# Weight loads in the order of use, vectors loaded as rows, and the second MLP's weights turned beside the first block, in an attention, MLP and LoRA-expert kernel on one core

## The chip, the cores and the metric

One core of a Trainium2 chip runs the whole program. Time is device microseconds (us) of one execution. What a measurement can tell from no change is said in the prediction. Engines are named as in the profile: PE is TensorE's matmul, PEld its weight load, DVE is VectorE, ACT is ScalarE, POOL is GpSimd, and SPq is the queue of SyncE, which issues every DMA of this kernel.

## What is computed

x is [4, 2048, 256] in float32: B = 4 batches, T = 2048 tokens, D = 256 features, 16 heads of 16. Weights are float32; MLP width is F = 1024.

```
xn  = ln(x) * g1 + b1n ;  q, k, v = split(xn @ w_in.T + b_in)
allowed = (idx % 8 == 0)[:, None] | (idx[:, None] == idx[None, :])
o   = softmax(where(allowed, q k^T / 4, -inf)) v
x1  = x + o @ w_out.T + b_out
x2  = x1 + gelu((ln(x1)*g2 + b2n) @ w1.T + b1) @ w2.T + b2
y   = layernorm(x + x2)
# second half: one of 8 experts is picked per token (top-1 of gate), each adds a rank-4 LoRA to the same wi
h   = relu(y @ wi.T + wi_b + (y @ A_e.T) @ B_e.T)
out = layernorm(y + h @ wo.T + wo_b)
```

Only one token in 8 attends to all tokens; the others see themselves alone, so for them attention is the value row itself. The kernel therefore works on a batch in 8 chunks of 256 tokens, one for each value of idx % 8. For chunks 1 to 7 attention is a matmul with v's and w_out's product; chunk 0 goes through real attention.

## The kernel before

**Precision.** Every float32 matmul is done as three matmuls of a reduced-width form (function `three`, lines 1459 to 1463 of the kernel): each operand is split into a high part, written by ACT, and a low part, written by DVE or POOL (exact value minus high part). So each weight tile needs a PE transpose ("turn"), one ACT copy, one DVE subtraction.

**Work of a batch.** It has two phases, *projection* and *attention*.
- Projection has three *pieces* for each of the 8 chunks (function `piece`): piece 0 normalises the next chunk (`pb`, DVE, tile xn) and multiplies k (`pk`, tile kst); piece 1 multiplies the first half of the value and x1 (`pv`), stores k (`stk`, 6 DMAs), takes the statistics of the chunk after next (`pa`, tile astats) and prepares x + the bias row on POOL (`xc`); piece 2 turns the next chunk (`pt`, tile xt), multiplies the second half, and completes x1 (`vx`: ACT writes vals, DVE adds into x1o, POOL sums x_s for the residual). `stx` stores x1 and x_s to DRAM, `ldx` loads a chunk of x into one of 4 buffers.
- Beside these run *items* of the two MLPs. A block is 512 tokens of one MLP ("M" the first, "F" the second) and has 8 items, one for each 128 of the 1024 hidden features: `up` (six matmuls of 512 columns, in the second MLP one more for the LoRA), gelu or relu on ACT (tile gel), `ev` (high part on ACT, low part on POOL: tile hid), and `dn` two items later. A block needs its rows normalised (`l2a`, `l2b`: tile x1in) and turned (`tn`: tile turned).
- `mx` steps (one PE pair and one DVE reduction each) find the maxima of the scores, in advance of the attention phase, which does `sc`, exponentials (tile prob) and `at` for 8 head pairs of 8 steps.

**Order.** `build_steps` writes one list of steps by hand; each engine walks through the whole list and issues its part in that order, so a wait in one step holds back everything behind it on that engine. `BANK` and `EARLIER` work out which PSUM bank a step uses and whom it waits for.

**The start.** SP loads four chunks of x, then all vectors and weights (`load_weights`, lines 719 to 740). Four vectors and wi_b are loaded as columns, one 4-byte element per partition (lines 722 to 724). Setup then makes the attention's weights: 6 of 25 groups (`wout`, `qk`, `vo`, `crow`), and the DVE products of `nwin` with the layer-norm bias (line 1148). The other 19 groups (`wt` steps 6 to 24: first MLP `upM`, `dnM`, second MLP `upF`, `dnF`, the gate `ga`, the LoRA `bst`) are put between the first 14 pieces, three or two ahead of each piece. The first MLP block of batch 0 starts after piece 14. It takes x1 of chunks 2 and 3 through DRAM: `stx` stores them and `l2l` loads them back into x1in. The first `up` waits for all 25 groups (line 1744 on):

```
                    if a == (0, 0):
                        pe.wait_ge(a_setup, A_SETUP)
                        pe.wait_ge(d_setup, D_SETUP)
```

The remaining 10 pieces go beside the first items, in shares of 3, 3, 2 and 2. The projection phase of batch 0 has three M blocks, 24 items, and 16 `mx` steps (`EARLY`).

## Time and profile before

| | |
|---|---|
| median of 3 runs | 1524.2 us (1523.08 to 1526.39) |
| the profiled execution | 1527.41 us, its span 1525.6 us |
| granted TensorE clock over the span | 0.985 of full speed |
| PE busy | 94% of the span |
| DVE, ACT, POOL busy | 55%, 48%, 43% |
| the first PE work after x's first chunk | at 15.77 us |
| the first `up` matmul | at 75.10 us |
| attention of batch 0 begins | at 179.91 us |

The page gives each engine's busy time over the span. It is an average over stages. The views read below are the table by stretches (busy time of each engine in a stretch, the granted clock, DMA share), the instructions in order of time, the groups by shape, and the waits (who waited for whom).

### The profile page before, as it was taken

The page shows a single profiled execution, that of the slowest core. Times are in us where ns is not written, and L with a number is a line of the kernel's source. Part 1 is how long each engine was busy: PE and PEld are TensorE (multiplying, and loading weights), DVE is VectorE, ACT ScalarE, POOL GpSimd, SP SyncE. Part 2 cuts the span into 40 slices and gives each one's busy share as a digit, 9 for nine tenths or more (in the row PEclk, how much of TensorE's full clock was granted, in tenths as well). Part 3 has the DMA queues.
Part 4 walks back from the last instruction along what each step waited for, and adds up shares of the span by engine and source line. Part 5 has one row for each costly group of instructions (what it writes and reads, how often), then busy time and mean ns, then how long its engine had stood idle before and what let it go on. Part 6 is the DMA issues. An engine that isn't in the chain of part 4 may idle for free.

```text
span 1525.6 us, 26433 instructions
## 1 busy us (share of the span) xinstructions
PE 1432.3 (94%) x10166; PEld 1074.9 (70%) x10166; DVE 839.0 (55%) x1791; ACT 725.3 (48%) x1071; POOL 649.9 (43%) x533
## 2 busy tenths in 40 slices
PE   5799899999989999999989999999999999999888
PEld 4587655568878765568878866566887765557777
DVE  6746466735645465545636545653575547663242
ACT  3353455554444555554434455455344455555433
POOL 2463321238754423235854431323775432133554
PEclk9899899999999999999999999999999999999999
DMA  8565123205561132212672213220567112310100
GB/s 199 172 194 118 36 47 75 53 15 191 188 143 55 36 76 47 53 42 77 201 200 60 77 25 75 51 54 15 163 203 156 56 36 48 76 25 28 43 15 28
DMA packets 102718, 131.55 MB, mean 86 GB/s; under 512 B 18889, under 2 KB 79249, under 8 KB 99473
## 3 DMA queue, kind: packets, MB, share of 16 engines
q1 hardware_dynamic: 102592, 129.86, 31.3%
q8 instruction: 81, 1.33, 0.4%
q14 instruction: 45, 0.36, 0.1%
HBM read 68.61 MB, written 61.10 MB: 85 GB/s over the span
## 4 chain that ended last, share of the span: by engine, by line
PE 72%; DVE 9%; POOL 6%; SPq 4%; DMA 4%; issue 3%; ACT 2%; POOLq 0%; DVEq 0%; ACTq 0%
PE ps L1461 17%; PE ps L1462 14%; PE ps L1463 14%; PE ps L1638 9%; PE ps L1627 6%; PE ps L1612 5%; DVE mx L1344 2%; PE ps L1683 2%; DMA k_d<-kst 2%; PE ps L1705 2%; DMA kslot<-ones_d 2%; SPq L770 1%; PE ps L1674 1%; POOL rows L961 1%; PE ps L1644 1%
## 5 line engine op out<-in xcount | busy, mean ns | idle before, releaser
L1344 DVE TENSOR_REDUCE mx<-ps 128x2 f32<-128x1024 f32 x256 | 313.3, 1224 | 265.9 <-PE ps L1612 252.2
L1082 ACT ACTIVATE prob<-ps 128x1024 f32<-128x1024 f32 x256 | 262.0, 1023 | 154.6 <-PE ps L1627 154.4
L974 POOL TENSOR_TENSOR hid0l<-gel,hid0h 128x512 fp32r<-128x512 f32 x86 | 112.5, 1308 | 232.2 <-ACT hid0h L1124 232.2
L974 POOL TENSOR_TENSOR hid1l<-gel,hid1h 128x512 fp32r<-128x512 f32 x85 | 111.1, 1307 | 228.0 <-ACT hid1h L1124 228.0
L974 POOL TENSOR_TENSOR hid2l<-gel,hid2h 128x512 fp32r<-128x512 f32 x85 | 111.1, 1307 | 217.3 <-ACT hid2h L1124 217.3
L1116 ACT ACTIVATE gel<-ps,cols 128x512 f32<-128x512 f32 x128 | 88.3, 690 | 197.4 <-PE ps L1463 188.8
L1638 PE MATMUL ps<-prob,vals 128*32 128x256 f32 x2048 | 165.4, 395 | 0.0
L1118 ACT ACTIVATE gel<-ps 128x512 f32<-128x512 f32 x128 | 76.6, 599 | 178.4 <-PE ps L1705 178.4
L1627 PE MATMUL ps<-qslot,kslot 50*128 50x256 f32 x1024 | 130.4, 333 | 7.1 <-ACT prob L1082 7.0
L1627 PEld LDWEIGHTS ps<-qslot,kslot 50*128 50x128 f32 x1024 | 77.2, 187 | 73.1 <-issue 47.9
L1612 PE MATMUL ps<-kslot,qslot 48*128 48x512 f32 x512 | 109.8, 425 | 9.6 <-DVE mx L1344 5.9
L1638 PEld LDWEIGHTS ps<-prob,vals 128*32 128x32 f32 x2048 | 40.5, 108 | 56.6 <-issue 47.1
L955 POOL TENSOR_TENSOR rstd<-vare,mhalf 128x4 f32<-128x4 f32 x47 | 50.2, 1068 | 69.5 <-DVE vare L1236 67.9
L961 POOL TENSOR_SCALAR rows<-rows,mv,rstd 128x256 f32<-128x256 f32 x60 | 73.6, 1238 | 0.0
L1419 DVE TENSOR_TENSOR rows<-rows,ps 128x512 f32<-128x512 f32 x62 | 40.6, 684 | 44.1 <-PE ps L1463 44.0
L1612 PEld LDWEIGHTS ps<-kslot,qslot 48*128 48x128 f32 x512 | 48.4, 185 | 22.0 <-DVE mx L1344 9.7
L1461 PE MATMUL ps<-turned1h,w1h 128*128 128x512 f32 x128 | 56.3, 440 | 5.6 <-DVE turned1l L1406 5.6
L1461 PE MATMUL ps<-turned0h,wih 128*128 128x512 f32 x128 | 60.2, 471 | 0.0
L1461 PE MATMUL ps<-turned0h,w1h 128*128 128x512 f32 x128 | 54.1, 422 | 4.0 <-DVE turned0l L1406 4.0
L1461 PE MATMUL ps<-turned1h,wih 128*128 128x512 f32 x128 | 57.7, 451 | 0.0
L911 POOL TENSOR_TENSOR arstd<-avare,mhalf 128x2 f32<-128x2 f32 x32 | 23.3, 729 | 76.7 <-DVE avare L1298 76.3
L1124 ACT ACTIVATE hid0h<-gel 128x512 fp32r<-128x512 f32 x86 | 54.2, 630 | 1.6
(238 smaller groups left out, 3968.5 us busy)
## 6 DMA issues: line engine op xcount, KB each, us to landing
k_d<-kst SPq DMA_DIRECT2D x192, 128.0 KB
kslot<-k_d SPq DMA_DIRECT2D x64, 384.0 KB
xin<-in_L_attn_x SPq DMA_DIRECT2D x32, 256.0 KB, 4.1
rows<-xs_d SPq DMA_DIRECT2D x16, 512.0 KB, 5.8
x1in<-x_d SPq DMA_DIRECT2D x15, 512.0 KB, 6.5
y_d<-rows SPq DMA_DIRECT2D x15, 512.0 KB, 3.1
rows<-y_d SPq DMA_DIRECT2D x15, 512.0 KB, 4.3
out<-rows SPq DMA_DIRECT2D x15, 512.0 KB, 4.5
```

The source lines that it names most:

```text
L961: nc.gpsimd.tensor_scalar(y[:, i, :], y[:, i, :], mv[:, k % 2, i, 0:1], rstd[:, k % 2, i:i + 1], ALU.subtract, ALU.mult).then_inc(final_do ...
L974: nc.gpsimd.tensor_tensor(hid[i % RING][1][:], gel[i % 2][:], hid[i % RING][0][:], ALU.subtract).then_inc(lo_done, 1)
L1082: nc.scalar.activation(prob[(n - 1) % 2][:].rearrange("p e i q -> p (e i q)"), ps[:, 0:2, :].rearrange("p a n -> p (a n)"), ACT.Exp).then_ ...
L1116: nc.scalar.activation(gel[i % 2][:], ps[:, UP, :], ACT.Gelu, bias=cols[:, B1C + f:B1C + f + 1]).then_inc(act_done, 1)
L1118: nc.scalar.activation(gel[i % 2][:], ps[:, UP, :], ACT.Relu).then_inc(act_done, 1)
L1344: nc.vector.tensor_reduce(best[:, :, j % NQ], ps[:, MX:MX + 2, :], AX.X, ALU.max).then_inc(maxr_done, 1)
L1461: mm(o, l[0], r[0], start=start, stop=False, skip_group_check=True)
L1462: mm(o, l[0], r[1], start=False, stop=False, skip_group_check=True)
L1463: return mm(o, l[1], r[0], start=False, stop=stop, skip_group_check=True)
L1612: last = mm(ps[:, MX + e, :], qslot[p % SLOTS][half, P * t:P * t + P], kslot[p % SLOTS][half, 512 * piece:512 * piece + 512], start=True, ...
L1627: last = mm(ps[:, e, QW * i:QW * i + QW], kslot[p % SLOTS][half, at:at + P], qslot[p % SLOTS][half, :], start=True, stop=True)
L1638: last = mm(ps[at:at + PR, OUT, 0:QW], vals[:, v:v + PR], prob[(n - 1) % 2][:, e, i, :], start=kk == 0, stop=kk == KK - 1)
```

## The change

1. **Loads.** The order on SP's queue becomes: chunk 2 of x, w_in and w_out, the vectors, then the second chunk of x, w1, w2, two more chunks of x, and last the second MLP's weights. Three `lw` steps replace the one `load_weights`.
2. **Vectors as rows.** ln1_g, ln2_g, b_in and b1 are loaded as 18 rows of 128 (tile vecs) and turned to columns by one PE transpose and one DVE copy. wi_b and lora_B are loaded with partition p holding features 8p to 8p+7, so in runs of 32 and 128 bytes in place of 4 and 16.
3. **x1 of the first block** (chunks 2 and 3 of batch 0) is summed by POOL and DVE directly in x1in. Their x1 stores and the first `l2l` load go.
4. **Turning.** Only the 8 groups of the first MLP are made between pieces; the block starts after piece 9 in place of 14. The other 11 groups (now dnF first, then upF) follow one after each of the items 0 to 10, all through PSUM bank 4. The first `up` waits for groups 0 to 13 only; the first gate product waits for all.
5. The remaining 15 pieces go beside items 0 to 5 (3, 2, 3, 2, 3, 2). Of batch 0's maxima 12 (`LEAD`) in place of 16 come before attention; the other 4 come with its first four steps. Batches 1 to 3 keep their order.

```diff
-FIRST, GROUPS = 6, 25
+FIRST, MEND, GROUPS = 6, 14, 25
...
-            if q + 2 < NA:
+            if q + 2 < NA and (b or q != 2):
...
-            left = list(range(FIRST, GROUPS))
-            for j in range(14):
-                for s in [("wt", left.pop(0)) for _ in range(min(3 if j < 5 else 2, len(left)))]:
+
+            now = {0: (6, 7), 1: (8, 9), 2: (10,), 3: (11,), 4: (12,), 5: (13,)}
+            for j in range(9):
+                piece(*todo.pop(0))
+                for g in now.get(j, ()):
+                    put(("wt", g))
+                for s in {5: [("l2a", k)], 6: [("l2b", k)], 7: [("tn", k, 0)], 8: [("tn", k, 1), ("pa", b, CHUNKS[4])]}.get(j, []):
                     put(s)
-                piece(*todo.pop(0))
-                for s in {8: [("l2l", k)], 10: [("l2a", k)], 11: [("l2b", k)], 12: [("tn", k, 0)], 13: [("tn", k, 1)]}.get(j, []):
-                    put(s)
-            share = [3, 3, 2, 2]
+            for j in range(MEND, GROUPS):
+                extra[j - MEND] = [("wt", j)]
+            share = [3, 2, 3, 2, 3, 2]
+            early = LEAD
...
+                    for s in {0 if j >= FT else 2: [("l2l", ready)], 3: [("l2a", ready)], 5: [("l2b", ready)], 6: [("tn", ready, 0)],
...
-    for q in range(XB):
-        put(("ldx", 0, CHUNKS[q]))
+    put(("ldx", 0, CHUNKS[0]))
+    put(("lw", 0))
+    put(("ldx", 0, CHUNKS[1]))
+    put(("lw", 1))
+    put(("ldx", 0, CHUNKS[2]))
+    put(("ldx", 0, CHUNKS[3]))
+    put(("lw", 2))
...
+def bank_of(k):
+
+    return k if k < FIRST else OUT + k % 4 if k < MEND else OUT
...
+def at_first(b, c):
+
+    return b == 0 and c // 2 == BLOCKS[0][2]
...
-    for w in ("M", "F"):
-        g += [("up" + w, i) for i in range(4)] + [("dn" + w, i) for i in range(4)]
+    g += [("upM", i) for i in range(4)] + [("dnM", i) for i in range(4)]
+    g += [("dnF", i) for i in range(4)] + [("upF", i) for i in range(4)]
...
+COLS, CVB = 2, 11
+BIAS_AT = 10
+    return CVB + 1 + min(k + 1, GROUPS - 2) + 9 * (k >= BIAS_AT) + 5 * (k >= GROUPS - 3)
...
+            def load_weights(part):
+                if part == 0:
+                    sp.dma_start(nwin[:], w_in.rearrange("(m p) d -> p m d", p=P)).then_inc(wload[0], 16)
+                    sp.dma_start(nwout[:], w_out.rearrange("(m p) d -> p m d", p=P)).then_inc(wload[1], 16)
+                        sp.dma_start(vecs[t:t + n, :], v.rearrange("(m p) -> m p", p=P)).then_inc(wload[3], 16)
+                    sp.dma_start(lnb[:, 0, :], rows_bc(ln1_b)).then_inc(wload[2], 16)
+                    sp.dma_start(boutr[:], rows_bc(b_out)).then_inc(wload[2], 16)
+                elif part == 1:
+                    sp.dma_start(nw1[:], w1.rearrange("(m p) d -> p m d", p=P)).then_inc(wload[4], 16)
+                    sp.dma_start(brow[:], rows_bc(b2)).then_inc(wload[11], 16)
+                    sp.wait_ge(p_const, 2 + E)
+                    sp.dma_start(ones_d.rearrange("h (k n) -> (h k) n", n=T // 16), vals[0:32, 0:T // 16]).then_inc(onesw, 16)
+                    sp.dma_start(lnb[:, 1, :], rows_bc(ln2_b)).then_inc(wload[10], 16)
+                    sp.dma_start(nw2[:], w2.rearrange("(m p) f -> p m f", p=P)).then_inc(wload[5], 16)
+                else:
+                    sp.dma_start(nwo[:], wo_W.rearrange("(m p) f -> p m f", p=P)).then_inc(wload[7], 16)
+                    sp.dma_start(nwi[:], wi_W.rearrange("(m p) d -> p m d", p=P)).then_inc(wload[6], 16)
+                    sp.dma_start(nga[0:E], gate_W).then_inc(wload[8], 16)
+                    sp.dma_start(nga[E:E + ER], lora_A.rearrange("e r d -> (e r) d")).then_inc(wload[8], 16)
+                    sp.dma_start(nlb[:], lora_B.rearrange("e (p m) r -> p e m r", p=P)).then_inc(wload[9], 16)
+                    sp.dma_start(wibc[:], wi_b.rearrange("(p m) -> p m", p=P)).then_inc(wload[9], 16)
+                    sp.dma_start(gateb[:], rows_bc(gate_b)).then_inc(wload[12], 16)
+                    sp.dma_start(wob[:], rows_bc(wo_b)).then_inc(wload[12], 16)
...
-                    sp.wait_ge(x1_done, N("stx", b, c))
-                    k, n = X1_STORE[(b, c)]
-                    sp.dma_start(x1_d[b, :, :, c, :], x1o[k][:]).then_inc(x1st[k], 16)
+                    if not at_first(b, c):
+                        sp.wait_ge(x1_done, N("stx", b, c))
+                        k, n = X1_STORE[(b, c)]
+                        sp.dma_start(x1_d[b, :, :, c, :], x1o[k][:]).then_inc(x1st[k], 16)
...
+                    sp.wait_ge(turn_done, N("tn", before("l2a", a[0])[1], 1))
                     if m == 1:
-
-                        sp.wait_ge(a_setup, A_SETUP)
-                        sp.wait_ge(d_setup, D_SETUP)
-                    if m > 1:
-                        sp.wait_ge(turn_done, N("tn", before("l2l", a[0])[1], 1))
+                        sp.wait_ge(xs_done, 2)
...
+                    x1 = tiles_of(x1in[:])[:, :, c % 2, :] if at_first(b, c) else x1o[(n - 1) % 2][:]
...
+                dve.wait_ge(vturn, 1)
+                link(nc.vector.tensor_copy(cols[:, 0:18], ps[:, 7, 0:18]))
+                assert chain[0] == COLS
...
-                    if b == FIRST:
+                    if b == BIAS_AT:
...
-                    dve.wait_ge(x1ld, 16 * N("l2l", *a))
+                    if a[0]:
+                        dve.wait_ge(x1ld, 16 * N("l2l", *a))
+                    else:
+                        dve.wait_ge(x1_done, 2)
...
+                pe.wait_ge(wload[3], 64)
+                pe.wait_ge(p_ident, 2)
+                nc.tensor.transpose(ps[:, 7, 0:18], vecs[:], ident[0:18, 0:18]).then_inc(vturn, 1)
...
+                        pe.wait_ge(a_setup, A_SETUP)
+                        pe.wait_ge(d_setup, D_SETUP)
-                        pe.wait_ge(a_setup, A_SETUP)
-                        pe.wait_ge(d_setup, D_SETUP)
+                        pe.wait_ge(a_setup, casts(MEND - 1))
+                        pe.wait_ge(d_setup, lows(MEND - 1))
```

How the order moves on three engines, row by row as a listing of the instructions gives it (line, operation, result<-operands, shape). **DVE**, from the end of setup: nw_142 is w1, xn, kst, xt and astats belong to a chunk, w1l, w2l and wil are low parts of weights. Before:

```order
L1170 TENSOR_TENSOR cols<-cols 128x8
L1200 SCALAR_TENSOR_TENSOR w1l<-ps,cols,w1h 128x512 x3
L1307 TENSOR_SCALAR xn_136<-xin_129,amv,arstd 128x256
L1307 TENSOR_SCALAR xn_137<-xin_129,amv,arstd 128x256
L1320 SCALAR_TENSOR_TENSOR kst_126<-ps,cols,kst_126 128x256 x2
L1200 SCALAR_TENSOR_TENSOR w1l<-ps,cols,w1h 128x512
L1209 TENSOR_TENSOR w2l<-ps,w2h 128x512 x2
L1293 BN_STATS astats<-xin_130 128x6 x2
L1296 BN_AGGR amv<-astats 128x2 x2
L1298 TENSOR_SCALAR avare<-amv 128x2
L1209 TENSOR_TENSOR w2l<-ps,w2h 128x512 x2
L1205 TENSOR_TENSOR wil<-ps,wih 128x512
```

Now:

```order
L1347 TENSOR_SCALAR xn_136<-xin_129,amv,arstd 128x256
L1347 TENSOR_SCALAR xn_137<-xin_129,amv,arstd 128x256
L1360 SCALAR_TENSOR_TENSOR kst_126<-ps,cols,kst_126 128x256 x2
L1238 SCALAR_TENSOR_TENSOR w1l<-ps,cols,w1h 128x512 x2
L1333 BN_STATS astats<-xin_130 128x6 x2
L1336 BN_AGGR amv<-astats 128x2 x2
L1338 TENSOR_SCALAR avare<-amv 128x2
L1238 SCALAR_TENSOR_TENSOR w1l<-ps,cols,w1h 128x512 x2
L1353 TENSOR_TENSOR xt1l<-ps,xt1h 128x512
L1370 TENSOR_TENSOR x1in<-x1in,ps 128x2x256
L1203 ISA junk,cols<-nw_142,lnb 128x256
```

The chunk's own work comes first and the eight bias products of w1 (line 1203, line 1168 before) come after it; x1 is summed in x1in.

**SPq**, its first issues. Before:

```order
L758 DMA xin_128<-in_L_attn_x 128x2x256
L758 DMA xin_129<-in_L_attn_x 128x2x256
L758 DMA xin_130<-in_L_attn_x 128x2x256
L758 DMA xin_131<-in_L_attn_x 128x2x256
L723 DMA cols<-in_L_attn_ln_g 128x2x1 x2
L723 DMA cols<-in_L_attn_b_in 128x6x1
L723 DMA cols<-in_L_attn_b 128x8x1
L724 DMA wibc<-in_L_ffn_wi_b 128x8x1
L725 DMA lnb<-in_L_attn_ln_b 128x256
L726 DMA nwin<-in_L_attn_w_in 128x6x256
L727 DMA boutr<-in_L_attn_b_out 128x256
L728 DMA nwout<-in_L_attn_w_out 128x2x256
```

Now:

```order
L784 DMA xin_128<-in_L_attn_x 128x2x256
L747 DMA nwin<-in_L_attn_w_in 128x6x256
L748 DMA nwout<-in_L_attn_w_out 128x2x256
L750 DMA vecs<-in_L_attn_ln_g 2x128 x2
L750 DMA vecs<-in_L_attn_b_in 6x128
L750 DMA vecs<-in_L_attn_b 8x128
L751 DMA lnb<-in_L_attn_ln_b 128x256
L752 DMA boutr<-in_L_attn_b_out 128x256
L784 DMA xin_129<-in_L_attn_x 128x2x256
L754 DMA nw_142<-in_L_attn_w 128x8x256
```

w_in (nwin) and w_out (nwout) move from the tenth and twelfth place up to the second and third; the second chunk of x moves from the second place to the tenth.

**ACT**, from the first gelu, in the change only (gel is the gelu's result, hid its high part, wfh the high part of the second MLP's down weights, kst, xt and vals belong to chunks):

```order
L1149 ACTIVATE gel_105<-ps,cols 128x512
L1076 ACTIVATE kst_127<-ps,cols 128x256 x2
L1157 ACTIVATE hid0h<-gel_105 128x512
L1064 ACTIVATE xt0h<-ps 128x512
L1085 ACTIVATE vals<-ps 128x32x16
L1036 ACTIVATE wfh<-ps 128x512
L1149 ACTIVATE gel_106<-ps,cols 128x512
L1076 ACTIVATE kst_126<-ps,cols 128x256 x2
L1157 ACTIVATE hid1h<-gel_106 128x512
L1036 ACTIVATE wfh<-ps 128x512
```

Before, the rows here were the same without wfh: one group is now made per item.

## Rows read from the trace of the kernel before

**Rows 1.** The page, part 1: busy us of each engine, share of the span, instructions.

```profile
PE 1432.3 (94%) x10166; PEld 1074.9 (70%) x10166; DVE 839.0 (55%) x1791; ACT 725.3 (48%) x1071; POOL 649.9 (43%) x533
```

**Rows 2.** Stretches: from:to, length, busy (count) of PE, PEld, DVE, ACT, POOL, PEclk, DMA, GB/s.

```profile
0.00:24.30 24.30, 8.14 (x33) 6.74 (x33) 11.04 (x37) 5.62 (x8) 6.09 (x18) 1.00 0.87 233
24.30:48.00 23.70, 17.87 (x122) 15.06 (x122) 23.11 (x59) 13.04 (x25) 7.79 (x7) 1.00 0.68 164
48.00:75.10 27.10, 19.67 (x90) 16.44 (x91) 19.04 (x48) 6.72 (x13) 11.82 (x11) 0.75 0.51 164
75.10:180.00 104.90, 97.24 (x591) 81.16 (x589) 60.10 (x117) 44.79 (x73) 54.16 (x44) 0.99 0.46 127
```

**Rows 3.** In order of time, SP's queue: start us, us of issuing, result<-operand, count.

```profile
0.73 2.65 SPq L758 DMA_DIRECT2D xin<-in_L_attn_x  x4
...
8.55 1.58 SPq L728 DMA_DIRECT2D nwout<-in_L_attn_w_out  x1
...
10.17 0.47 SPq L729 DMA_DIRECT2D brow<-in_L_attn_b  x1
```

**Rows 4.** In order of time, setup on PE and DVE: start, us, [idle before <-releaser].

```profile
15.77 1.11 PE L1473 MATMUL ps<-ident,nwout 128*128 128x128 f32 x4 [7.67 <-DMA nwout<-in_L_attn_w_out]
...
16.68 0.42 DVE L1148 CUSTOM_DVE_ANT_0 junk<-nwin,lnb 128x256 f32<-128x256 f32 x1 [5.94 <-issue]
...
23.78 0.42 DVE L1190 TENSOR_TENSOR crow<-ps,boutr 128x256 f32<-128x256 f32 x1
...
33.44 0.75 DVE L1293 BATCH_NORM_STATS2 astats<-xin 128x6 f32<-128x256 f32 x2
...
34.51 0.17 DVE L1298 TENSOR_SCALAR avare<-amv 128x2 f32<-128x2 f32 x1
```

**Rows 5.** The page, part 6: loads of a chunk of x, KB each, median us to landing.

```profile
xin<-in_L_attn_x SPq DMA_DIRECT2D x32, 256.0 KB, 4.1
```

**Rows 6.** Groups by shape, DVE, 0 to 72 us: count | busy us, mean ns | idle before.

```profile
L1307 DVE TENSOR_SCALAR xn<-xin,amv,arstd 128x256 f32<-128x256 f32 x12 | 7.0, 622 | 0.9 <-POOL arstd L911 0.9
...
L1320 DVE SCALAR_TENSOR_TENSOR kst<-ps,cols,kst 128x256 fp32r<-128x256 f32 x10 | 4.3, 475 | 2.2 <-ACT kst L1043 2.2
L1168 DVE CUSTOM_DVE_ANT_0 junk<-nw,lnb 128x256 f32<-128x256 f32 x8 | 3.4, 426 | 0.3
L1200 DVE SCALAR_TENSOR_TENSOR w1l<-ps,cols,w1h 128x512 fp32r<-128x512 f32 x4 | 2.8, 746 | 0.0
...
L1209 DVE TENSOR_TENSOR w2l<-ps,w2h 128x512 fp32r<-128x512 f32 x4 | 2.6, 686 | 0.0
```

**Rows 7.** In order of time, before and at the first `up`: DVE and PE.

```profile
57.84 2.36 DVE L1307 TENSOR_SCALAR xn<-xin,amv,arstd 128x256 f32<-128x256 f32 x2
...
64.31 1.41 DVE L1222 BATCH_NORM_STATS2 stats<-x1in 128x6 f32<-128x256 f32 x4 [0.28 <-DMA x1in<-x_d]
...
66.16 0.17 DVE L1236 TENSOR_SCALAR vare<-mv 128x4 f32<-128x4 f32 x1
...
68.47 2.33 DVE L1243 TENSOR_SCALAR x1in<-x1in,mv,rstd 128x256 f32<-128x256 f32 x4 [0.96 <-POOL rstd L955]
...
75.10 0.64 PE L1461 MATMUL ps<-turned0h,w1h 128*128 128x512 f32 x1
```

**Rows 8.** Waits of PE from 48 to 75.1 us: us in total, times, longest.

```profile
PE ps L1461 <- DVE xt0l L1313: 4.7, 1, 4.7
```

**Rows 9.** In order of time, PE: twelve turns of 128 columns, and two neighbouring 512-column matmuls.

```profile
38.71 1.47 PE L1473 MATMUL ps<-ident,nwo 128*128 128x128 f32 x12
...
58.38 0.40 PE L1462 MATMUL ps<-wal,xt1h 128*128 128x512 f32 x1
58.61 0.39 PE L1463 MATMUL ps<-wah,xt1l 128*128 128x512 f32 x1
```

**Rows 10.** Waits of PE from 75.1 to 182 us, the longest.

```profile
PE ps L1689 <- DVE us L1276: 3.8, 1, 3.8
```

**Rows 11.** In order of time, PE: the second score step of batch 0.

```profile
183.00 0.80 PE L1627 MATMUL ps<-qslot,kslot 50*128 50x256 f32 x4 [2.30 <-ACT prob L1082]
```

151 lines of the change are left out of this document (70 added, 81 removed).

## The prediction

> **What bounds the kernel now.** I read the page first, then the table by stretches, then the start in order of time. Over the span PE is busy 94% [rows 1], so elsewhere only fewer PE cycles would help, and the change touches nothing there: batches 1 to 3 keep their order. The table by stretches shows where PE is not full [rows 2]. From 0 to 24.3 us it is busy 8.1 us, from 24.3 to 48.0 17.9 of 23.7, from 48.0 to 75.1 19.7 of 27.1, and from 75.1 to attention at 180.0 97.2 of 104.9. So 75 us pass before the first `up`, and in them 29 us of PE time are empty. What fills them is different in each stretch:
> - Until 24.3 us the loads. w_out was issued at 8.55 and PE had it at 15.77; DVE's setup began at 16.68, when the vectors (brow, issued at 10.17, was the last of those it asks for) were there, and ended with crow at 24.2 [rows 3, 4]. That is 7.5 us of DVE work.
> - From 24.3 to 48.0 DVE is busy 23.1 of 23.7 us [rows 2]: it is the bound, with the low parts of all weights.
> - After that, waits: x1 comes back from DRAM, DVE can take its statistics at 64.3 only, and the one long wait of PE (4.7 us) ends with a DVE instruction queued behind them [rows 7, 8]. PE's granted clock falls to 0.75 of 2.4 GHz in this stretch [rows 2].
>
> **The change, part by part.** I work out three times: the end of setup, the first `up`, and the start of attention. What follows attention is unchanged, so the gain at that point is the gain at the end.
>
> *End of setup.* In the new queue the second chunk of x is what DVE's setup comes behind (its statistics stand ahead of it in the list). It is issued tenth. Before, twelve issues took from 0.73 to 8.55 us [rows 3], 0.65 each, so it is issued at 0.73 + 9 x 0.65 = 6.6 and lands 4.1 later [rows 5], at 10.7. Its statistics take 1.2 (33.44 to 34.68) [rows 4], the new copy of the columns and fold 0.4 (two of DVE's small instructions, an estimate), then the 7.5 us as before: setup ends at 19.8, not 24.2. Bounds: if it lands as late as w_out did, 7.2 us after the issue [rows 3, 4], 22.9; if in 2.8 us, 18.5. The PE turn of 18 rows costs a fraction of a turn (0.12) [rows 9] and ends before DVE needs it: nothing. It replaces loads of single elements; I count no more for them than the earlier landing.
>
> *First `up`.* DVE stays the bound, now with 9 pieces and 8 groups in place of 14 and 19. Its list, at busy time by count [rows 6]: 3 chunks of xn at 2 x 0.58 = 3.5; kst 3 x 0.87 = 2.6; statistics of two chunks 2 x 1.24 = 2.5 [rows 4]; groups 4 x 0.70 + 4 x 0.65 = 5.4; three xt and three x1 of the same shape as w2l, 6 x 0.65 = 3.9; eight bias products with their read-outs 3.9 (3.4 and 0.06 each, an estimate); l2a 2.0 (64.31 to 66.33) and l2b 2.3 [rows 7]; one turned0l 0.65. Sum 26.8. DVE cannot run gapless: the first kst waits for twelve matmuls and ACT (2 us), the last normalised rows for PE's turn and ACT (2 us). I take 4; the bounds are 2 and 10 (the stretch from 48.0 to 75.1 had 8 us of DVE idle [rows 2]). The trip of x1 through DRAM is gone, and nothing takes its place: x1in is summed 7 us before it is wanted. First `up`: 19.8 + 26.8 + 4 = 50.6, against 75.1: 24.5 us earlier.
>
> *Attention.* Most of that is work put off, and from here PE is full. Before, the rest took 104.9 us [rows 2]. Now it also holds 5 more pieces and 11 groups, and 4 maxima less. Neighbouring 512-column matmuls start 0.23 apart, 256 columns I take as half, and a turn as 0.12 [rows 9]. The pieces hold two pk (12 of 256 columns: 1.4 each), three half pv (6 of 512: 1.4 each) and one pt (0.5): 7.5. The groups hold 42 turns: 5.1. The maxima: 4 x 2 x 0.235 = 1.9. Net 10.7. DVE, ACT and POOL have room for their part: in this stretch they are busy 60, 45 and 54 of 105 us [rows 2], and DVE gets 11 low parts and the LoRA's copies, some 11 us. PE's largest wait there, 3.8 us for DVE's pick [rows 10], stays. Attention begins at 50.6 + 104.9 + 10.7 = 166.2, not 180.0: 13.8 us earlier.
>
> *The four maxima* now run with the first score steps. There PE stood 2.3 us waiting for an exponential [rows 11], so half of their 1.9 us is hidden: +0.9. Nothing hidden would be +1.9, and all hidden 0.
>
> *What is hidden and costs nothing:* the moved loads of the second MLP (needed after item 0, at 50 us), the single bank of the 11 groups (an item and its pieces lie between two of them), and SP's queue, which has fewer issues.
>
> The sum is -13.8 + 0.9 = -12.9. The profiled execution took 1527.4 us (span 1525.6), 3.2 above the median of the runs shown; it would become 1514.5, and the median 1524.2 becomes **1511**.
>
> **Two rules weighed.** PE in the new stretch from 19.8 to 50.6 has 3 chunks of 4.7 us and 8 groups of 0.5, 18 of 31 us, or 58%, thinner than the 75% that held 1.00 and the 73% that got 0.75 [rows 2]. The Trainium skill ("TensorE: Matmul & The Clock Gate", the part on the HAM clock gate) says that the array runs at 1.2 GHz until it has been busy for a while, and falls back after idling. That speaks against thinning PE out here, and is the first rival. The second: two xn took 2.36 us while POOL worked and 1.17 on average [rows 6, 7]. By the Trainium skill ("SBUF — State Buffer", Who interferes with whom) a DVE instruction with two SBUF inputs blocks against a POOL instruction that reads SBUF; the eight bias products have two, and POOL now works beside them. By that rule they would cost about one POOL sum more. The sum without it stands.
>
> **The rivals.**
> - *PE drops to 1.2 GHz in the new first stretch.* Then its parts on the chain double: the first pk 1.4, a pt with a half pv 1.9, and at the end a turn, a pt and a half pv 2.4: +5.7, so 1517. For it: 58% busy. Against: DVE, not PE, bounds most of it. 0.15.
> - *The maxima hold attention up.* Each keeps both banks until DVE's reduction ends, so the four could cost their whole cycle (0.5 + 1.2) on PE: 6.8 in place of 0.9, 1517. 0.08.
> - *The loads come no earlier*, since the bytes ahead are what counts and not the place in the queue: setup stays at 24.2, 4.4 less gained, 1515. 0.07.
> - *More is gained:* setup at 18.5 and PE's 7.7 us of gaps from 75.1 to 180.0 half filled by the denser work: -1.3 - 3.9, 1506. 0.12.
> - *Slower: the 11 groups in one bank stall PE.* If PE came to the next user of bank 4 before ACT's copy and DVE's subtraction (about 0.65 each [rows 6], with hand-overs 1.6) each time, 11 x 1.6 = 17.6 us, and 1529. It decides from 1.2 us per group on (12.9 / 11). Against it: PE has 3 to 7 us of work between two groups. 0.04.
>
> **How the numbers follow.** The forecast has the remaining 0.54, from 1507 to 1515 by the bounds of setup (-1.3, +3.1) and of DVE's waits (-2, and +1 to +3 of the +6 that the bound allows). Range: 1505 to 1518 takes in every case but the slower one and tails of the others. A change within 0.2% (3 us, 1521.2 to 1527.2) is about what a measurement of this kernel can't tell from none. Faster by more: 0.92; within: 0.04; slower: 0.04.
>
> **What the changed profile would show.** Right: first PE group near 8 us; DVE's crow ends at 19 to 21; first matmul on turned0h and w1h at 49 to 53, behind a DVE that is over 85% busy; no wait for x1in in block 0; from there to the first score matmul about 115.6 us with PE at 93% or more; everything after that as long as before. Wrong: PE's clock near 0.5 or 0.75 from 20 to 50; waits of PE on w or wf low parts beside items; PE waits on `mx` in the first score steps; or a later stretch that has changed its length, which nothing here explains.

## The result, and the profile after

| | before | change |
|---|---|---|
| median beside each other | 1524.7 us (1523.08 to 1526.39, 4 runs) | 1516.14 us (1515.72 to 1516.53, 4 runs) |
| ratio, with 95% interval | | 0.9937 [0.9917, 0.9957] |
| profiled execution, span | 1527.41 us, 1525.6 us | 1515.91 us, 1514.1 us |
| granted clock over the span | 0.985 | 0.987 |
| setup ends (end of crow) | 24.20 us | 18.83 us |
| first `up` matmul | 75.10 us | 51.74 us |
| attention of batch 0 | 179.91 to 331.74 us | 169.85 to 320.47 us |
| last matmul | 1518.0 us | 1506.5 us |

The kernel is faster by 8.6 us, where 13 were predicted. By the marks the gain is 5.4 us at the end of setup, 23.4 at the first `up`, 10.1 at the start of attention and 11.3 at its end. From there to the last matmul it is 1186.0 us in place of 1186.3, so the change did its work before 320 us, as foreseen.

The page of the kernel after, part 1, answers to [rows 1]: busy us of each engine, share of the span, instructions.

```profile
PE 1426.0 (94%) x10167; PEld 1071.3 (71%) x10167; DVE 837.3 (55%) x1792; ACT 725.7 (48%) x1071; POOL 649.9 (43%) x533
```

The table by stretches of the kernel after, with the columns of [rows 2]: setup, up to the first `up`, up to attention, and the first twice 10 us of attention.

```profile
0.00:18.80 18.80, 8.58 (x33) 6.77 (x33) 11.10 (x37) 5.71 (x8) 6.09 (x18) 1.00 0.89 284
18.80:51.70 32.90, 22.47 (x123) 19.22 (x124) 25.40 (x67) 10.74 (x21) 12.80 (x11) 0.84 0.52 160
51.70:169.80 118.10, 107.14 (x670) 91.14 (x668) 71.80 (x153) 54.97 (x91) 61.34 (x50) 0.99 0.48 133
169.80:179.80 10.00, 8.13 (x54) 3.95 (x54) 4.69 (x5) 5.97 (x6) 0.00 (x0) 0.63 0.01 2
179.80:189.80 10.00, 9.83 (x84) 5.74 (x82) 6.38 (x9) 5.73 (x8) 1.30 (x1) 1.00 0.08 18
```

The same twice 10 us in the kernel before, from the start of its attention on:

```profile
179.90:189.90 10.00, 7.59 (x44) 3.45 (x43) 0.64 (x4) 5.78 (x6) 0.00 (x0) 0.50 0.01 3
189.90:199.90 10.00, 9.83 (x84) 5.90 (x80) 4.45 (x5) 5.33 (x9) 1.29 (x1) 0.92 0.00 0
```

What to see: in the second stretch DVE is busy 25.4 of 32.9 us, so it idles 7.5; PE's granted clock is 0.84 there. In the third, PE's busy time grew against [rows 2] by 9.9 us (97.24 to 107.14) and its gaps from 7.7 to 11.0 us. Attention begins at half the clock in both kernels, and how long that lasts differs.

The kernel after in order of time, setup on SP's queue, PE and DVE (start, us, [idle before <-releaser]); it answers to [rows 3, 4].

```profile
4.92 0.58 SPq L784 DMA_DIRECT2D xin<-in_L_attn_x  x1
...
11.78 5.57 SPq L763 DMA_DIRECT2D nga<-in_L_ffn_gate_W  x1
...
8.41 1.12 PE L1518 MATMUL ps<-ident,nwout 128*128 128x128 f32 x4
...
9.84 0.75 DVE L1333 BATCH_NORM_STATS2 astats<-xin 128x6 f32<-128x256 f32 x2 [0.39 <-DMA xin<-in_L_attn_x]
...
11.33 0.42 DVE L1183 CUSTOM_DVE_ANT_0 junk<-nwin,lnb 128x256 f32<-128x256 f32 x1
...
18.42 0.41 DVE L1228 TENSOR_TENSOR crow<-ps,boutr 128x256 f32<-128x256 f32 x1
```

The second chunk of x is issued at 4.92 and DVE has it at 9.84; from 11.33 the setup of 7.5 us follows without a gap. PE turns w_out at 8.41 instead of 15.77.

The kernel after in order of time, four places of the new first stretch, on DVE, POOL and PE; it answers to [rows 7].

```profile
29.08 1.40 DVE L1203 CUSTOM_DVE_ANT_0 junk<-nw,lnb 128x256 f32<-128x256 f32 x1
...
30.52 0.43 DVE L1203 CUSTOM_DVE_ANT_0 junk<-nw,lnb 128x256 f32<-128x256 f32 x1
...
28.80 1.39 POOL L964 TENSOR_TENSOR xin<-xin,x1in 128x512 f32<-128x512 f32 x1
...
44.02 3.29 DVE L1281 TENSOR_SCALAR x1in<-x1in,mv,rstd 128x256 f32<-128x256 f32 x4
...
47.45 1.09 PE L1722 MATMUL ps<-ident,x1in 128*128 128x128 f32 x4 [5.53 <-DVE x1in L1281]
48.34 1.06 PE L1626 MATMUL ps<-ident,xn 128*128 128x128 f32 x4
...
51.74 0.48 PE L1506 MATMUL ps<-turned0h,w1h 128*128 128x512 f32 x1
```

Behind DVE's x1in PE stands 5.5 us, and the four turns after that take 1.09 us, as they do at half the clock.

The longest waits of DVE in the kernel after, 18.8 to 51.7 us (us in total, times, longest):

```profile
DVE kst L1360 <- ACT kst L1076: 2.1, 1, 2.1
DVE turned0l L1451 <- ACT turned0h L1122: 1.9, 1, 1.9
DVE w1l L1238 <- ACT w1h L1033: 1.0, 1, 1.0
```

The waits of PE in the kernel after, 51.7 to 172 us, against [rows 10]:

```profile
PE ps L1740 <- DVE us L1316: 3.8, 1, 3.8
PE ps L1722 <- DVE wil L1243: 1.9, 1, 1.9
PE ps L1506 <- DVE turned0l L1451: 1.7, 2, 0.9
PE ps L1722 <- ACT wih L1033: 1.5, 1, 1.5
```

The two that name wil and wih are new. There the transposes of a later block (`tn`) wait for bank 4, in which a weight group still stands. The score steps, against [rows 11]:

```profile
169.85 0.79 PE L1675 MATMUL ps<-qslot,kslot 50*128 50x256 f32 x4
...
172.94 0.80 PE L1675 MATMUL ps<-qslot,kslot 50*128 50x256 f32 x4 [1.87 <-ACT prob L1115]
```

### The profile page after: what moved, and what is told of

Its sections match the earlier page's. It is cut to its first block, busy times and chain, and to the rows that moved or that the text cites. A ratio compares the mean times of both kernels' runs of the same rounds, so it can differ in the third digit from the quotient of the medians.

```text
span 1514.1 us, 26426 instructions
## 1 busy us (share of the span) xinstructions
PE 1426.0 (94%) x10167; PEld 1071.3 (71%) x10167; DVE 837.3 (55%) x1792; ACT 725.7 (48%) x1071; POOL 649.9 (43%) x533
## 4 chain that ended last, share of the span: by engine, by line
PE 75%; DVE 10%; POOL 4%; SPq 3%; DMA 3%; issue 3%; ACT 2%; POOLq 0%; DVEq 0%; ACTq 0%
PE ps L1506 18%; PE ps L1507 15%; PE ps L1508 15%; PE ps L1686 9%; PE ps L1675 6%; PE ps L1660 5%; DVE mx L1384 2%; PE ps L1734 2%; PE ps L1756 2%; PE ps L1722 2%; POOL rows L992 1%; DMA k_d<-kst 1%; PE ps L1692 1%; DMA kslot<-ones_d 1%; SPq L796 1%
## 5 line engine op out<-in xcount | busy, mean ns | idle before, releaser
L1157 ACT ACTIVATE hid2h<-gel 128x512 fp32r<-128x512 f32 x85 | 53.5, 630 | 1.6
```

What stands on the lines that cost most here:

```text
L1157: nc.scalar.activation(hid[i % RING][0][:], gel[i % 2][:], ACT.Copy).then_inc(hi_done, 1)
```

## The experiments

Twelve runs were made; e8 and e11 repeat a kernel. The marks below are read from each run's own profile as in the table above. "Its length" is the attention of batch 0 from the start of its first score step to that of its last, and "rest" is from there to the last matmul, in which e1 to e5, e8 and e9 leave all as it is, and e6, e7 and e10 to e12 move steps of later batches with the same edit. Ratios are to the kernel before on the same chip.

| run | ratio, 95% interval | median us | setup ends | first `up` | attention starts | its length | rest |
|---|---|---|---|---|---|---|---|
| before | | 1524.7 | 24.20 | 75.10 | 179.91 | 151.8 | 1186.3 |
| change | 0.9937 [0.9917, 0.9957] | 1516.14 | 18.83 | 51.74 | 169.85 | 150.6 | 1186.0 |
| e8, change again | 0.9969 [0.9954, 0.9985] | 1520.75 | 18.34 | 51.20 | 169.10 | 150.7 | 1192.0 |
| e1, five groups in bank 0 | 0.9921 [0.9897, 0.9944] | 1514.69 | 18.33 | 51.21 | 168.04 | 155.3 | 1186.7 |
| e2, all groups before `up` | 0.9953 [0.9933, 0.9973] | 1520.81 | 18.32 | 68.50 | 175.45 | 152.7 | 1187.5 |
| e3, vectors as columns | 0.9970 [0.9953, 0.9986] | 1522.88 | 22.48 | 56.97 | 176.09 | 153.4 | 1189.1 |
| e4, before with 12 maxima | 0.9985 [0.9966, 1.0004] | 1525.18 | 24.88 | 76.60 | 178.45 | 152.2 | 1184.8 |
| e5, x chunks first | 0.9953 [0.9938, 0.9968] | 1519.31 | 20.49 | 53.78 | 173.28 | 150.6 | 1186.7 |
| e6, picks behind the gate | 0.9934 [0.9921, 0.9947] | 1516.93 | 18.55 | 52.72 | 167.25 | 153.3 | 1187.2 |
| e7, three moves | 0.9905 [0.9886, 0.9924] | 1513.07 | 18.66 | 49.88 | 161.02 | 151.3 | 1184.3 |
| e11, three moves again | 0.9903 [0.9883, 0.9922] | 1511.46 | 18.80 | 50.17 | 163.59 | 151.7 | 1184.8 |
| e9, x1 through DRAM | 0.9969 [0.9954, 0.9984] | 1523.44 | 18.34 | 59.35 | 174.50 | 153.5 | 1183.6 |
| e10, `up` between all scores | 1.0035 [1.0019, 1.0051] | 1531.57 | 18.50 | 50.87 | 165.10 | 164.9 | 1201.2 |
| e12, one `up` in the wait | 0.9858 [0.9837, 0.9879] | 1505.57 | 18.55 | 51.58 | 165.00 | 148.5 | 1187.1 |

How far one profile's mark can be trusted shows where the order is the same. The change, e8 and e6 have one order up to the first `up`, and it came at 51.2 to 52.7 us. e7, e11 and e12 have one order up to attention, which began at 161.0, 163.6 and 165.0. The rest is the same in the change, e8, e3, e5 and e9, and took 1183.6 to 1192.0 us. The times are no finer: the ratios of e2, e3, e5 and e9 (0.9953 to 0.9970) lie between the change's two (0.9937, 0.9969) or beside them. So what e2, e3, e5 and e9 say of each part's share rests on marks, and only differences beyond these spreads are told apart.

### Where the miss could sit: e1 to e4

**e1.** The last five groups are turned in bank 0, which the transposes don't use.

```diff
-    return k if k < FIRST else OUT + k % 4 if k < MEND else OUT
+    return k if k < FIRST else OUT + k % 4 if k < MEND else OUT if k < 20 else 0
```

> The changed kernel, but the last five of the 11 groups (20 to 24) are turned in PSUM bank 0, which no piece uses any more, and not in bank 4, which the block turn tn uses. In the changed kernel two tn of block 1 wait 1.9 and 1.5 us for a group's low part and high part. Theory A (bank 4 is what costs): these 3.4 us go, attention starts at 166.5 us and not at 169.85, and the time is 1512.7. Rival B (PE would wait elsewhere for the same DVE and ACT work, behind which the tn copies queue as well): the waits move to the turned1 tiles, attention starts at 169 or later, the time stays at 1516.

Two waits of PE from 51.2 to 170 us in e1:

```profile
PE ps L1506 <- DVE turned0l L1451: 1.7, 2, 0.9
PE ps L1722 <- DVE x1in L1281: 1.3, 1, 1.3
```

The waits for wil and wih (3.4 us together) are gone, and one of 1.3 us for x1in has come. From the first `up` to attention it took 116.8 us, 1.3 less than the change: a third of what the waits summed to. The ratio can't be told from the change's. Attention itself was 155.3 us long; the two stretches from its start say why (columns of [rows 2]):

```profile
168.00:178.00 10.00, 8.13 (x44) 4.09 (x43) 3.83 (x4) 5.08 (x6) 0.00 (x0) 0.50 0.01 2
178.00:188.00 10.00, 10.00 (x57) 5.74 (x56) 4.42 (x7) 4.48 (x6) 0.00 (x0) 0.55 0.00 1
```

From the start of attention PE is at half the clock for some 18 us, where the change was for 7. No part of that attention differs between the two kernels. It is this clock, not the bank, that made a later look at the start of attention necessary (e6, e7, e10 to e12).

**e2.** The fourth part is undone: all 19 groups and 14 pieces before the first `up`, 16 maxima before attention.

```diff
-            for j in range(9):
+            left = list(range(FIRST, GROUPS))
+            for j in range(14):
+                for s in [("wt", left.pop(0)) for _ in range(min(3 if j < 5 else 2, len(left)))]:
+                    put(s)
                 piece(*todo.pop(0))
...
-            share = [3, 2, 3, 2, 3, 2]
-            early = LEAD
+            share = [3, 3, 2, 2]
+            early = EARLY
```

> The changed kernel with its part 4 undone: all 19 groups lie between the first 14 pieces as before, 16 maxima come before attention; loads, rows and x1 in x1in stay as changed. Theory A (the work put off is what gives most, as the prediction's sum has it): DVE's list before the first up grows by some 19 us, first up near 71, attention at 71 + 104.8 = 176, time near 1521. Rival B (loads, rows and the missing trip of x1 give most, and putting work off only moves it): first up near 67, attention at 171 to 172, time 1517 or less.

Attention starts at 175.45, 4.5 us before that of the kernel before and 5.6 behind the change's. By this mark loads, rows and x1 give less than half, and turning the second MLP's weights beside the first block gives the rest, with the four maxima, which e2 puts back too (1.5 us in e4). Theory A held: attention was expected at 176 and the time near 1521.

**e3.** The four vectors that the change loads as rows (ln1_g, ln2_g, b_in, b1) are loaded as columns again; wi_b and lora_B stay as they are in the change.

```diff
-                    for t, v, n in ((G1, ln1_g, KT), (G2, ln2_g, KT), (BIN, b_in, 6), (B1C, b1, FT)):
-                        sp.dma_start(vecs[t:t + n, :], v.rearrange("(m p) -> m p", p=P)).then_inc(wload[3], 16)
+                        for t, v, n in ((G1, ln1_g, KT), (G2, ln2_g, KT), (BIN, b_in, 6), (B1C, b1, FT)):
+                            sp.dma_start(cols[:, t:t + n], v.rearrange("(m p) -> p m", p=P)).then_inc(wload[3], 16)
```

> The changed kernel, but the four vectors are loaded as columns of single elements again, at the same place in the queue (no PE turn, the DVE copy goes to unused columns). Theory A (the single elements hold the DMA engines): in the kernel before, the engines moved under 65 GB/s for 3 us while they were loaded; w_out and x's second chunk land 3 to 4 us later, setup ends near 22 and not at 18.8, time 1519. Rival B (they only cost descriptors beside other loads): setup ends within 0.5 us of 18.8, time 1516.

The stretch from 6 to 12 us of e3, two issues on SP's queue, and DVE's statistics of the second chunk, in order of time:

```profile
6.00:12.00 6.00, 5.03 (x21) 4.48 (x22) 1.43 (x3) 1.79 (x3) 0.14 (x1) 1.00 0.73 148
```

```profile
5.61 1.85 SPq L752 DMA_DIRECT2D lnb<-in_L_attn_ln_b  x1
...
7.98 0.58 SPq L785 DMA_DIRECT2D xin<-in_L_attn_x  x1
```

```profile
13.50 0.75 DVE L1334 BATCH_NORM_STATS2 astats<-xin 128x6 f32<-128x256 f32 x2 [4.07 <-DMA xin<-in_L_attn_x]
```

The same stretch of the change:

```profile
6.00:12.00 6.00, 4.92 (x21) 4.39 (x22) 3.45 (x13) 2.40 (x5) 0.85 (x2) 1.00 1.07 326
```

With 2304 elements of 4 bytes in the queue the DMA engines moved 148 GB/s, without them 326. The chunk came 3.7 us later. Most of that is the issue and not the transfer: the chunk was issued at 7.98 instead of 4.92 us, 3.1 later, behind slower issues of the vectors and of lnb (1.85 us), and its landing took 5.5 instead of 4.9. Setup ended 3.65 later, and attention started 6.2 later than the change's. I had counted nothing for this beyond the earlier landing. By the mark at attention it is the largest piece, but e2's 5.6 lies within the spread of such marks, so this order isn't shown; at the end of setup, where the change and e8 agree within 0.5 us, it is clear.

**e4.** On the kernel before, only the number of maxima ahead of batch 0's attention is changed.

```diff
             share = [3, 3, 2, 2]
+            early = LEAD
...
-                if d >= 0 and (mine[0] < EARLY) and (d % 3 != 2 or n - j <= EARLY - mine[0]):
+                if d >= 0 and (mine[0] < early) and (d % 3 != 2 or n - j <= early - mine[0]):
```

> The kernel before with one thing changed: batch 0 has 12 maxima before attention and the other 4 with its first steps. Theory A (the prediction's): 1.9 us less PE work before attention, half of it back inside: attention starts 1.9 earlier at 178.0, lasts 0.9 longer, time 1.0 less, 1523.7. Rival B (what the two traces show: attention of batch 0 lasted 150.6 us with 12 and 151.8 with 16): attention starts 1.9 earlier and is 1.2 shorter, time 1521.6. Rival C (the maxima hold up the first score steps): time 1525 or more.

From the first `up` to attention it took 101.8 us instead of 104.8, and the attention 152.2 instead of 151.8: 3.0 saved, 0.4 given back. But e4's first `up` came 1.5 us late with the same order up to it, so attention starts only 1.5 us earlier (178.45), near the 178.0 of theory A. The interval of the ratio includes 1, so the times don't show it either.

### The loads and the trip through DRAM: e5 and e9

**e5.** Rows stay, but all four chunks of x go ahead of the weights again.

```diff
-    put(("ldx", 0, CHUNKS[0]))
+    for q in range(XB):
+        put(("ldx", 0, CHUNKS[q]))
     put(("lw", 0))
-    put(("ldx", 0, CHUNKS[1]))
     put(("lw", 1))
-    put(("ldx", 0, CHUNKS[2]))
-    put(("ldx", 0, CHUNKS[3]))
     put(("lw", 2))
```

> The changed kernel with the first part alone undone in its order: the four x chunks are asked for ahead of all weights again, and then the three groups of weights. Everything else stays. Theory A (the order of use is worth what the wait of the first output-weight transpose was): in the kernel before, 4 chunks of x of 0.26 MB stand ahead of the weights; 1 MB at the 284 GB/s of the first 18.8 us of the changed kernel is 3.7 us, of which the first chunk's share (0.9 us) stays, so w_in and w_out land 2.8 us later, the end of the setup comes at 21.5 to 22 us instead of 18.8, and the attention of batch 0 at 172.5 instead of 169.85; the time is 2 to 3 us above the change (some 1518.5), and DVE gets its first statistics no later. Rival B (rows for columns do it all; DMAs of 128 KB and more are never what is waited for, since ScalarE's casts and VectorE's chain of 4 us between the landing and the first transposes hide it): setup end within 1 us of 18.8, the time within 1 us of the change.

In order of time, PE in e5:

```profile
11.61 0.29 PE L1562 MATMUL ps<-ident,vecs 18*128 18x18 f32 x1 [3.53 <-DMA vecs<-in_L_attn_b]
```

PE waits 3.5 us for the rows, and turned them at 8.19 us in the change. Setup ends 1.7 to 2.2 us later than in the two profiles of the change, attention starts 3.4 to 4.2 later. The mark is short of theory A at the setup and past it at attention; the time, 1519.3, lies between the two medians of the change and decides nothing. By the end of setup the order matters less than the rows (3.65 us in e3).

**e9.** x1 of the first block goes through DRAM, and the block starts behind 12 pieces.

```diff
-    return b == 0 and c // 2 == BLOCKS[0][2]
+    return False
...
-            for j in range(9):
+            for j in range(12):
...
-                for s in {5: [("l2a", k)], 6: [("l2b", k)], 7: [("tn", k, 0)], 8: [("tn", k, 1), ("pa", b, CHUNKS[4])]}.get(j, []):
+                for s in {6: [("l2l", k)], 8: [("l2a", k), ("pa", b, CHUNKS[4])], 9: [("l2b", k)], 10: [("tn", k, 0)], 11: [("tn", k, 1)]}.get(j, []):
```

> The changed kernel with the third part undone: x1 of the first block goes through DRAM again (VectorE sums in x1o, a store, a load into the MLP's buffer), and since that transfer has to be waited for, the first normalization and the transposes stand three pieces later and the first `up` behind 12 pieces instead of 9; rows, load order and the late groups stay. Theory A (this part is what makes nine pieces possible, and no more): the first `up` comes three pieces, some 7 to 8 us, later than 51.2, at 59; these pieces are missing behind it, so the attention starts within 1 us of the change's 169.1 if the transfer is hidden; the wait of 5.5 us for x1in of the changed kernel goes or shrinks, as more pieces lie between the sums and the transpose, and the attention comes even 1 to 3 us earlier. Rival B (the transfer is not hidden): TensorE waits 3 us or more for x1in behind the load, and the attention comes 2 to 5 us later. The time then is that of the change less 1 to 3 (A) or plus 2 to 5 (B).

SP's load and DVE's statistics in e9 in order of time, and its longest wait of PE from 18.4 to 59.4 us:

```profile
43.57 0.57 SPq L875 DMA_DIRECT2D x1in<-x_d  x1
```

```profile
47.98 1.41 DVE L1259 BATCH_NORM_STATS2 stats<-x1in 128x6 f32<-128x256 f32 x4 [2.77 <-DMA x1in<-x_d]
```

```profile
PE ps L1716 <- DVE x1in L1280: 7.9, 1, 7.9
```

Rival B held: the transfer isn't hidden, DVE stands 2.8 us for it, PE 7.9 instead of 5.5, and attention starts 5.4 us behind e8's. So the third part is what lets the block start behind nine pieces without a longer wait; with the trip through DRAM only this one order of 12 pieces was run.

### Is it the same from run to run: e8

> The changed kernel once more, unchanged, on the same chip and beside the same runs of the kernel before as the three others, so that they can be compared with it, and with a second profile of it. Theory A (the stages cost what they cost, and only the stretches behind a wait differ in their clock): marks up to the start of the attention of batch 0 within 0.5 us of the first profile (18.8, 51.7, 169.85), and the granted clock over the 10 us behind the 3.8 us wait anywhere from 0.5 to 1.0, with the first attention stage 150.6 to 155 us long by it; time 1513 to 1518. Rival B (it is all the same from run to run): every stage within 0.5 us of the first profile, the clock behind the wait 0.63 again.

The marks up to the attention are within 0.8 us of the first profile and its stage within 0.1. But the rest is 6.0 us longer, with the same number of matmuls. The rest of e8, of the change's first profile, and of the kernel before (columns of [rows 2]):

```profile
319.80:1511.80 1192.00, 1148.67 (x8112) 873.03 (x8112) 629.72 (x1353) 568.04 (x842) 536.31 (x427) 0.99 0.30 81
```

```profile
320.50:1506.50 1186.00, 1141.52 (x8112) 867.89 (x8112) 629.43 (x1353) 567.54 (x842) 535.65 (x427) 0.99 0.30 81
```

```profile
331.70:1518.00 1186.30, 1142.59 (x8113) 869.04 (x8112) 631.04 (x1353) 568.35 (x842) 536.21 (x427) 0.99 0.30 81
```

PE is busy 7.2 us longer for the same work, DVE 0.3, and the granted clock over the span was 0.983, for 0.987 in the first profile: it is PE's clock, not the order. Twelve timed executions of e8 show it as well: from 1515.7 us at a granted clock of 0.987 to 1527.4 at 0.977. A straight line through all 76 executions of the kernel before that ran beside these experiments falls 1.1 us per 0.001 of clock, one through the 16 of the change 1.2. At 0.987 the lines stand at 1525.1 and 1517.1 us: 8.0 us apart. Theory A was wrong in two things: it expected the spread at the start of attention, and in e8 it lay behind it; and it expected 1513 to 1518 us, where the median is 1520.75. Why half of e8's executions were granted 0.984 or less stays open. It isn't the chip: the kernel before had 0.982 to 0.988 beside them.

The line also lets other kernels be compared. If each execution is set against it at its own clock, the kernels lie below it by these means: the change 9.0 and 7.2 us (e8), e1 and e6 10.0, e7 12.1, e11 13.0, e12 14.4; e2, e3 and e5 6.1 to 6.4, and e9 4.8. e10 lies 4.3 above it; e4, with one execution at a clock of 0.936, is left out. This takes away what an order gains by a higher clock. Undoing a part then costs 1.3 to 2.9 us against the mean of the change's 16 executions (7.7), less than the marks of e2, e3, e5 and e9 say, and why stays open.

### What is left to take: e6, e7, e10, e11 and e12

**e6.** Both halves of the expert choice right behind the gate product.

```diff
-                    for s in {3: [("tn", ready, 0)], 4: [("tn", ready, 1), ("xw", ready)], 5: [("ga", ready)],
-                              6: [("pick", ready, 0), ("pick", ready, 1)], 7: [("pi", ready)]}.get(f, []):
+                    for s in {3: [("tn", ready, 0)], 4: [("tn", ready, 1), ("xw", ready)], 5: [("ga", ready), ("pick", ready, 0), ("pick", ready, 1)],
+                              7: [("pi", ready)]}.get(f, []):
```

> The changed kernel with both halves of the expert choice (`pick`, 12 short VectorE instructions of 5.9 us) put right behind the gate product in the items of the projection, ahead of one maximum, instead of an item later. In the changed kernel the gate's copy was there at 158.7 us and the first pick instruction ran at 162.8, behind a maximum that itself waited for TensorE; TensorE then waited 3.8 us for the last one (`us`) before it could go on to the attention of batch 0, with the clock at half for the 10 us behind it (0.63 from 169.8 to 179.8). Theory A (that wait is the queue's, and the clock falls because of the wait): the wait is at most 0.5 us, the granted clock stays at 1.0 over the start of the attention, the time is 3.3 us of the wait and 2 to 4 us of the clock below the change: 5 to 7 us less, 1509 to 1511. Rival B (only the wait goes, the clock falls there anyway because PE's work at the start of the attention has gaps of its own, 2.30 us for the exponent): the attention starts 3 to 3.5 us earlier and the first 10 us stay at 0.5 to 0.65; 3 to 3.5 us less. Rival C (the maxima pushed behind the picks hold TensorE's next score step up, since its bank waits for the maximum): a wait for `mx` of 2 to 4 us appears at 160 to 166 and the time is the same as the change.

PE's longest wait from 150 to 172 us in e6, the 5 us ahead of attention, the first 5 us of it, and its first twice 10 us:

```profile
PE ps L1675 <- ACT prob L1115: 2.0, 2, 1.8
```

```profile
162.20:167.20 5.00, 5.00 (x32) 3.85 (x30) 3.73 (x7) 1.95 (x3) 2.18 (x2) 1.00 0.19 65
167.20:172.20 5.00, 2.67 (x24) 1.29 (x24) 3.12 (x3) 3.93 (x4) 2.96 (x3) 0.92 0.00 0
167.20:177.20 10.00, 7.67 (x49) 3.73 (x51) 4.71 (x5) 5.60 (x6) 2.96 (x3) 0.71 0.00 1
177.20:187.20 10.00, 9.83 (x73) 5.48 (x65) 5.36 (x8) 5.19 (x8) 1.29 (x1) 0.78 0.00 1
```

The 5 us ahead of attention in the change:

```profile
164.80:169.80 5.00, 1.15 (x6) 0.66 (x4) 4.83 (x5) 0.00 (x0) 3.61 (x3) 0.72 0.00 0
```

The wait for `us` is gone and nothing in its place, so attention starts 2.6 and 1.9 us earlier than in the two profiles of the change. The clock falls all the same (rival B), but later: in the change it fell during the 3.8 us wait (0.72 over the 5 us ahead of attention), in e6 it is still 0.92 over the first 5 us of attention and falls behind the next wait, the 1.8 us for the exponent. The stage is 153.3 us long and ends where the change's ended. So in the profile either wait is followed by a stretch at half the clock, and taking away the first only moves the fall to the second. In time e6 gained: its median is 3.8 us below e8's on the same chip (ratios 0.9934 and 0.9969, intervals apart), 2.8 at equal clock, though not the 5 to 7 of theory A.

**e7 and e11.** e6's move, e1's bank, and the first transpose of block 0 moved behind the ninth piece.

```diff
-                for s in {5: [("l2a", k)], 6: [("l2b", k)], 7: [("tn", k, 0)], 8: [("tn", k, 1), ("pa", b, CHUNKS[4])]}.get(j, []):
+                for s in {5: [("l2a", k)], 6: [("l2b", k)], 8: [("tn", k, 0), ("tn", k, 1), ("pa", b, CHUNKS[4])]}.get(j, []):
```

> The changed kernel with three moves at once: the picks right behind the gate product; the last five groups of weights turned in bank 0 instead of the bank of the transposes (the two waits `tn` <- VectorE wil and ScalarE wih of 1.9 and 1.5 us went with it in an earlier run); and the first input transpose of block 0 put behind the ninth piece, next to the second, so that TensorE does the 2 transposes and the value products of that piece while it would wait 5.5 us for x1in. Theory A (the waits are separate and each falls by what it is): 5 to 7 from the picks, 1.3 from the bank, 2 to 3.5 from the transpose (the value products and the transposes of that piece are 2.4 us at full clock): 8 to 11 below the change, 1505 to 1508. Rival B (work that fills a wait is work that then runs at the half clock, and the next wait, for the x1in of the second transpose, takes the place): the transpose move gives under 1 us, and the sum is 5 to 7 below. Rival C (the spread of the clock decides, not the waits): no difference from e6 beyond 1 us.

> The kernel with the three moves once more, on the same chip as the two others. Theory A (the gain is there whatever the chip): ratio 0.988 to 0.993 to the kernel before, marks within 0.7 us of the first profile (18.7, 49.9, 161.0). Rival B (the first profile was a lucky one): the ratio is that of the change, 0.9937 to 0.997.

Attention starts at 161.0 and 163.6 us, 8 and 5.5 before e8's, and the two ratios, 0.9905 and 0.9903, stand below both of the change's. The gain in ratio repeats; e7's mark at attention doesn't (e11 is 2.6 us later, where 0.7 was expected), so the sum of 8 to 11 us held in one profile of two. In time the gain is 7.7 us against e8 on the same chip, of which 4.9 at equal clock, and 1505 to 1508 us was missed (1513.07 and 1511.46). Which of the three moves gives what isn't told apart by times. Ahead of the first `up` the transpose does what was meant: PE's wait of 5.5 us for x1in became one of 2.0, with one of 1.4 for turned0l behind it. The first `up` is 1.0 to 1.9 us earlier in e7 and e11 than in the two profiles of the change, but e12 with the same order has it at 51.58, so that this gain is within the spread. The start of e7's attention is still at a clock of 0.66:

```profile
161.00:171.00 10.00, 7.91 (x52) 3.73 (x51) 4.67 (x5) 5.39 (x6) 2.95 (x3) 0.66 0.01 2
```

**e10.** The three moves, and every score step of a two-block attention two quarters later.

```diff
-        ahead = 2 if len(blocks) == 2 else 0
+        ahead = 0
```

> The kernel with the three moves, and a fourth: at the start of the attention of two blocks the first `up` of the expert block stands behind the first score step, where now three score steps and two of weighted sums come first. TensorE waited 1.8 us there for the first exponent (ACT_TABLE_LOAD of 1.28 us and prob of 1.02), right where its clock fell to half for some 10 us in every profile so far (0.50 to 0.59 over 5 to 15 us). Theory A (the clock falls for what is waited for around that start): with 1.4 us of `up` per half item in the wait, the granted clock stays at 1.0 or is at half for under 5 us, the first attention stage is 146 to 149 us long instead of 151.3, and the time is 3 to 5 us under the three moves. Rival B (the score steps are then late for the rest of the stage, as the later ones lie two quarters behind, and ScalarE has less ahead): the clock is as before, attention stages are the same or up to 2 us longer each, the time is the same or up to 4 us more.

The longest wait of PE over the whole of e10:

```profile
PE ps L1675 <- DMA qslot<-mT: 13.2, 13, 2.5
```

A miss: the stages of batches 0 and 3 became 164.9 and 165.9 us long, where even rival B allowed 2 us more each. The two steps of lead had hidden a transfer of each pair's maxima into qslot; without them PE waits for it. The start bears on theory A all the same. Three matmuls of `up` stood in the wait for the exponent, 0.9 us of it was left, and the clock was at half for under 4 us. The first 10 us:

```profile
165.10:175.10 10.00, 8.81 (x58) 5.06 (x57) 4.44 (x4) 5.93 (x7) 0.41 (x1) 0.83 0.00 1
```

**e12.** The three moves, and only the first `up` put into the first wait; the lead stays.

```diff
-            while s < STEPS_B and s * 4 * n <= (quarter + ahead) * STEPS_B:
+            while s < STEPS_B and s * 4 * n <= (quarter + ahead) * STEPS_B and not (ahead and s == 1 and quarter < 2):
```

> The kernel with the three moves, and of the fourth only the start: in an attention of two blocks (batches 0 and 3) both halves of the first `up` of the expert block stand behind the first score step, in the 1.8 us for which TensorE waits for the first exponent; the second to the fifth score step follow, and from there on the order is that of the three moves, so that nothing is late for its transfer (with the whole stage moved, TensorE waited 13.2 us for qslot, and the stages of batch 0 and 3 were 164.9 and 165.9 us long in place of 151.3 and 149.9). Theory A (a filled wait keeps the clock): the granted clock in the 10 us from the start of the attention is over 0.9 where it was 0.65 to 0.66, the stage is 148 to 149.5 us long, the time 2 to 3 us under the three moves. Rival B (the halves of `up` only take the place: their 1.4 us at half clock are 2.8, and the clock falls anyway): the stage is within 1 us of 151.3, the time the same. Rival C (something else in the moved order comes late, as before): the stage is over 153 us long.

e12 at the start of attention, PE in order of time, and the stretch of 10 us from there:

```profile
165.82 0.50 PE L1660 MATMUL ps<-kslot,qslot 48*128 48x512 f32 x2 [0.32 <-DVE mx L1384]
166.25 0.50 PE L1506 MATMUL ps<-turned1h,wih 128*128 128x512 f32 x1
...
167.75 0.39 PE L1756 MATMUL ps<-ust,bst 98*128 98x512 f32 x1
168.09 0.50 PE L1675 MATMUL ps<-qslot,kslot 50*128 50x256 f32 x4
```

```profile
165.00:175.00 10.00, 8.77 (x71) 4.42 (x71) 6.78 (x9) 7.49 (x8) 2.96 (x3) 1.00 0.01 3
```

Where PE stood 1.8 us it now runs seven matmuls, and no wait in these 10 us is longer than 0.4 us. The granted clock is 1.00 over them, the only profile here in which it is. The stage is 148.5 us long, 2.8 less than e7's. So theory A held for the clock and the stage. The kernel took 1505.57 us (1501.31 to 1510.02, 4 runs), 0.9858 of the kernel before: 1.4% against the change's 0.3 to 0.6%. That is 5.9 to 7.5 us below the three moves, where 2 to 3 were expected; at equal clock it is 1.4 to 2.3. The four executions were granted 0.989 to 0.994, those of the kernel before on the same chip 0.984 to 0.987, so the chip isn't the reason. The stretch at the start of one attention accounts for part of the higher clock, and where the rest of it comes from isn't shown: batch 3's stage, with the same move, stayed at 149.8 (149.9 in e7), and in the one profile of e12 attention begins later and the rest is longer than in e7's.

## Why the prediction was right in direction and too large

- **End of setup: right, 0.97 us better.** Predicted 19.8, measured 18.83. The issue of the second chunk came at 4.92 instead of 6.6, since the nine issues ahead of it took 0.47 us each and not 0.65; its landing took 4.9 instead of 4.1. Statistics and the 7.5 us are as counted. The step that had no price was "I count no more for them than the earlier landing": the vectors as columns had held up the issues behind them, 3.65 us at the setup and 6.2 at attention (e3).
- **First `up`: 51.74 against 50.6.** DVE's list was 26.8 and measured 25.4 busy. Its idle time was the mis-sized term: 4 taken, 7.5 measured, within the bounds of 2 and 10. Three waits for ACT (2.1, 1.9, 1.0) make most of it. "No wait for x1in in block 0" was wrong: the sum was early, but PE needs DVE's normalised rows, which came last in DVE's list.
- **The clock rival came half true.** PE's clock was 0.84 in the stretch, at half near both of its ends. The Trainium skill ("TensorE: Matmul & The Clock Gate", the part on the HAM clock gate) says that the array falls back after idling, and the rows agree: behind the 5.5 us wait four turns took 1.09 us and the next four 1.06, where four took 0.60 at 51.39, just ahead of the first `up`. As DVE bounds the stretch, its price can't be more than the 3.5 us by which DVE idled longer than counted, and not the 5.7 of the rival.
- **The port.** One bias product took 1.40 us, the other seven about 0.43, and POOL's sum of 1.39 us ran beside the slow one; x1in's four took 3.29 us beside two POOL sums, 2.33 before [rows 7]. That is what the Trainium skill says ("SBUF — State Buffer", Who interferes with whom) of an instruction with two SBUF inputs, and its cost is 1 us, somewhat less than one sum. For x1in's, whose column operands I had not counted as such, the rows show the same delay without settling its reason.
- **From the first `up` to attention: this is the step that failed.** 115.6 predicted, 118.1 measured. PE's busy time rose by 9.9 us (10.7 counted), but its gaps by 3.3 and not by nothing. The term "the single bank of the 11 groups (an item and its pieces lie between two of them)" was given no cost; it had two waits of 1.9 and 1.5 us, for the transposes share the bank. e1 took them away and got back 1.3. With the earlier first `up` falling 1.1 short too, attention began 10.1 us earlier, and not 13.8.
- **The four maxima: about as counted.** -1.9 ahead of attention and +0.9 in it were predicted. e4 has attention 1.5 us earlier (3.0 less from the first `up`, which came 1.5 later) and 0.4 longer. In the change the stage was even 1.2 us shorter, beside a higher clock at its start (0.63 and then 1.00, for 0.50 and then 0.92).
- **The base.** The sum was -12.9, the profiles say -11.5, and the medians -8.6. I subtracted from a profiled execution at a clock of 0.985, and carried the 3.2 us by which it stood above its median over to the change. The change's profile stood at its median. What nothing touched also moved: the projection of batch 2 was 2.9 us shorter (183.2 and 180.3), that of batch 3 and its attention 1.1 and 1.2 longer, which nearly cancel. At equal clock the gain is 8.0 us.
- **Slower by the bank:** its mechanism exists, at 3.4 us in all and not 17.6.
- **The signs.** Setup ended just ahead of the 19 to 21 named (18.83), and three more of those named as right were missed: DVE was 77% busy ahead of the first `up` (25.4 of 32.9 us) and not over 85%, PE waited for x1in in block 0, and from there to attention PE was 91% busy (107.14 of 118.1) and not 93. One of those named as wrong appeared, a wait on a low part (wil). The last four belong to the two terms above, DVE's idle time and PE's gaps.
- **What was luck.** The total landed in the range partly by cancelling: setup 1.0 us better than the sum and the stage 2.1 better, against 2.1 lost ahead of the first `up`, 2.5 behind it, and the base.

## What to carry to other kernels

Price a bad access pattern in a load queue by what stands behind it, not by its own landing: 2304 elements of 4 bytes brought the chunk of x behind them 3.7 us later, 3.1 of it at its issue. Behind a wait of PE count the clock as well as the wait, look for the next wait that would take its place (e6), and fill the wait with work that is ready (e12: 2.8 us from a 1.8 us wait, in one profile), but keep the lead that hides transfers (e10). And before a gain of under 1% is believed, compare executions at the same granted clock, since here 0.001 of it is 1.1 us.

## What the runs showed of the hardware that was not expected

- PE's clock around the start of attention was at half for some 3 to 20 us in every profile but e12's, also where the attention is the same: 0.63 and then 1.00 over twice 10 us in the change, 0.50 and 0.55 in e1. With a 3.8 us wait ahead of the attention the fall came in that wait or within 1 us of the attention's start; without it (e6, e7, e11) it came in the 1.8 us wait for the exponent or 1 us behind it; with that wait half filled (e10, 0.9 us left) it lasted under 4 us; with both filled (e12) it didn't come. Whether e12 would do so in every execution one profile can't show; its four times (granted clock 0.989 to 0.994 over the span, for 0.977 to 0.988 in the change's and 0.985 to 0.992 in those of e7 and e11) speak for it.
- Before 18.8 us the granted clock reads 1.00, and still four turns took 1.12 us at 8.41, twice the 0.60 of 51.39. So that reading doesn't show everything that slows PE; what does it there wasn't tried.
- In one of the two profiles of the change the same 8112 matmuls of the rest took PE 7.2 us more.
- One DMA issue on SP's queue took 5.57 us, that of the gate's weights, with the DMA engines' share at 1.03 to 1.07. No wait for a load behind it shows in the trace. In the kernel before the same issue took 1.46 us.
